# The first steps of a feed-forward stage: bias rows loaded in two parts, the last block's statistics and the next tile's transposes moved earlier

## The reference, cut to what matters

```python
Xd = _quant_dequant_fp8(X)                     # X = layernorm(x), bf16, 2048 x 512
D = Xd @ W0d.T + bias0.astype(jnp.float32)     # 2048 x 1792
D = jax.nn.gelu(D, approximate=False)
Dd = _quant_dequant_fp8(D.astype(bf16))
E = Dd @ W1d.T + bias1.astype(jnp.float32)     # 2048 x 512
x = x + E
```

## Time and profile before

| | us |
|---|---|
| median of 3 runs | 1640.8 (1638.39 to 1643.19) |
| the profiled execution's own time | 1641.23 |
| its span, first to last instruction | 1639.5 |
| PE, DVE, ACT, POOL busy in it | 1485.9, 1267.8, 858.3, 305.9 |

### The profile page before, as it was taken

How to read it: one execution, slowest core, us unless ns; L and a number is a source line. 1 busy time by engine, 2 the same in 40 slices (tenths; PEclk the granted TensorE clock), 3 DMA queues, 4 the chain that set the end, 5 groups by cost and what they waited for, 6 DMA issues and landing times. The chain is left out here.

```text
span 1639.5 us, 29417 instructions
## 1 busy us (share of the span) xinstructions
PE 1485.9 (91%) x11227; PEld 780.1 (48%) x11227; DVE 1267.8 (77%) x2276; ACT 858.3 (52%) x1776; POOL 305.9 (19%) x271
## 2 busy tenths in 40 slices
PE   6999999999999999999999887799999987777695
PEld 4455455455545554555555443344444444443253
DVE  4877876777677677777777786899888886999777
ACT  3554552343424434434334332688888854888552
POOL 0032130011111102010111100011111103789620
PEclk9999999999999999999999998899999999999898
DMA  6287573214231231414132223122232340876402
GB/s 243 83 173 164 128 169 85 78 52 104 58 97 51 64 102 35 130 27 115 51 102 64 52 103 117 24 45 46 45 62 50 59 97 5 154 110 110 76 1 103
DMA packets 317143, 140.73 MB, mean 86 GB/s; under 512 B 265856, under 2 KB 290560, under 8 KB 316800
## 3 DMA queue, kind: packets, MB, share of 16 engines
q1 hardware_dynamic: 273936, 98.14, 28.3%
q10 hardware_dynamic: 43120, 41.42, 8.3%
HBM read 66.13 MB, written 11.53 MB: 47 GB/s over the span
## 5 line engine op out<-in xcount | busy, mean ns | idle before, releaser
L638 PE MATMUL xp<-WO,OT 128*128 128x512 f16 x1536 | 340.4, 382 | 4.1 <-DVE X L925 4.1
L599 PE MATMUL pj<-XT,WQ 128*128 128x512 f16 x1536 | 338.9, 380 | 5.5 <-DVE WQ L284 4.9
L638 PEld LDWEIGHTS xp<-WO,OT 128*128 128x128 f16 x1536 | 148.3, 98 | 187.3 <-issue 16.2
L599 PEld LDWEIGHTS pj<-XT,WQ 128*128 128x128 f16 x1536 | 148.1, 98 | 181.6 <-issue 7.1
L756 ACT ACTIVATE E<-E 128x512 f32<-128x512 f32 x64 | 40.2, 628 | 300.8 <-DVE E L902 300.8
L1163 PE MATMUL db<-W0T,XD 128*128 128x448 f16 x768 | 156.7, 363 | 15.9 <-DVE XD L1361 11.0
L925 DVE SCALAR_TENSOR_TENSOR X<-xp,X 128x512 f32<-128x512 f32 x128 | 88.2, 689 | 91.1 <-PE xp L638 90.1
L1181 PE MATMUL eb<-W1T,DT 128*128 128x512 f16 x672 | 149.2, 382 | 4.2 <-ACT eb L1268 4.2
L573 POOL TENSOR_TENSOR VW<-VW,XB 128x1024 f32<-128x1024 f32 x14 | 33.0, 2356 | 615.0 <-DVE VW L102 615.0
L862 DVE SCALAR_TENSOR_TENSOR QT<-pj,QT 128x512 f16<-128x512 f32 x128 | 87.9, 687 | 70.8 <-ACT QT L726 70.8
L1163 PEld LDWEIGHTS db<-W0T,XD 128*128 128x128 f16 x768 | 75.7, 100 | 94.6 <-DVE XD L1361 12.0
(11 more groups left out here) (239 smaller groups left out, 2465.7 us busy)
## 6 DMA issues: line engine op xcount, KB each, us to landing
W0T<-in_L_xattn_wo ACTq DMA_DIRECT2D x15, 1024.0 KB, 5.5
W0T<-in_L_xattn_wq SPq DMA_DIRECT2D x9, 1024.0 KB, 5.5
W0T<-in_L_xattn_wq ACTq DMA_DIRECT2D x7, 1024.0 KB, 5.6
X<-in_x SPq DMA_DIRECT2D x4, 1024.0 KB, 7.6
out<-X SPq DMA_DIRECT2D x8, 512.0 KB, 3.6
XB<-in_L_ffn_W ACTq DMA_DIRECT2D x28, 128.0 KB, 3.0
w0t<-XB ACTq DMA_DIRECT2D x7, 512.0 KB, 7.4
w1t<-W0T ACTq DMA_DIRECT2D x7, 512.0 KB, 7.9
```

Source lines behind the costliest of these rows:

```text
L599: last = pe.matmul(bank[:, :], w, src[:, b, k, tokens], start=n == 0, stop=n == 3 * KC - 1)
L638: last = pe.matmul(xp[i % 2][:, :], OT[:, a, j, i * P:(i + 1) * P], WO[:, b, j, :], start=n == 0, stop=n == 3 * REP - 1)
```

## The change

1. Each bias is loaded in two transfers: row 0 into partition 0, and the same row into partitions 1 to 127. SP issues the two single rows first (semaphore `row_ld`), then the two others (`b_ld`), then `W1T`. The bias matmuls of tile 0 contract over partition 0 alone and wait for `row_ld`. The first `seed_d` waits for both semaphores.
2. In steps 0 and 1 PE transposes the next tile behind the first quarter of `first_product`, not behind the fourth. ACT's `high_x` and DVE's `low_x` of these steps stand earlier in their streams.
3. The five pieces of block 3 are made in steps -1, 0, 0, 0 and 1. ACT's square root stands in step 0, ahead of the first gelu.
4. In the first attention one semaphore, `sum_step`, takes the place of two.

The core of the diff:

```diff
+                 "exp_done pj_hi e_hi ot_hi max_done sub_done sum_step p_done pj_lo e_lo ot_lo x_acc "
             def sums(cur, jp):
-                at = count(cur, 2, jp + 1)
-                dve.wait_ge(S["exp_done"], at)
-                dve.reduce_sum(ST[:, 1, jp, :], E[:, jp, :, :], AX.X).then_inc(S["sum_done"], 1)
-                dve.wait_ge(S["sum_done"], at)
-                dve.reciprocal(ST[:, 2, jp, :], ST[:, 1, jp, :]).then_inc(S["rcp_done"], 1)
+                dve.wait_ge(S["exp_done"], count(cur, 2, jp + 1))
+                dve.reduce_sum(ST[:, 1, jp, :], E[:, jp, :, :], AX.X).then_inc(S["sum_step"], 1)
+                dve.wait_ge(S["sum_step"], count(cur, 4, 2 * jp + 1))
+                dve.reciprocal(ST[:, 2, jp, :], ST[:, 1, jp, :]).then_inc(S["sum_step"], 1)
...
         @block.sync
-            sp.dma_start(B0[:, :], b0.partition_broadcast(P)).then_inc(S["b_ld"], 16)
-            sp.dma_start(B1[:, :], b1.partition_broadcast(P)).then_inc(S["b_ld"], 16)
+            for row, b in ((B0, b0), (B1, b1)):
+                sp.dma_start(row[0:1, :], b.partition_broadcast(1)).then_inc(S["row_ld"], 16)
+            for rest, b in ((B0, b0), (B1, b1)):
+                sp.dma_start(rest[1:P, :], b.partition_broadcast(P - 1)).then_inc(S["b_ld"], 16)
...
-                        pe.matmul(db[q][:, 0:NQ], ones[:, :], B0[:, q * NQ:(q + 1) * NQ], start=True, stop=False)
+                        pe.matmul(db[q][:, 0:NQ], ones[0:1, :], B0[0:1, q * NQ:(q + 1) * NQ], start=True, stop=False)
...
-                    pe.wait_ge(S["b_ld"], 32)
+                    pe.wait_ge(S["row_ld"], 32)
+
+                soon = fixed(i) in (0, 1)
                 if live(i):
-                    first_product(i, range(4))
+                    first_product(i, range(1) if soon else range(4))
                 if live(nxt):
                     transpose_x(nxt)
+                if soon:
+                    first_product(i, range(1, 4))
...
             def seed_d(i, qs):
                     if fixed(i) == 0 and q == 0:
                         act.wait_ge(S["b_ld"], 32)
+                        act.wait_ge(S["row_ld"], 32)
...
                     x_times_rec(after)
+                if fixed(i) == 0:
+                    stats_x(act, 3)
+                if fixed(i) in (0, 1):
+                    high_x(nxt)
...
-                if live(nxt) and fixed(i) != -1:
+                if live(nxt) and fixed(i) not in (-1, 0, 1):
                     high_x(nxt)
...
-                if fixed(i) == X3_STEPS[1]:
-                    stats_x(act, 3)
...
                     quant_x(after)
+                if fixed(i) == -1:
+                    x_moments(dve, 3)
+                if fixed(i) in (0, 1):
+                    low_x(nxt)
+                if fixed(i) == 0:
+                    x_statistics(dve, 3)
                 if live(hidden):
                     off_grid_d(hidden)
...
+                if fixed(i) == 0:
+                    x_normal(dve, 3)
                 if live(i):
                     amax_d(i, 1)
...
                     scales_d(i)
+                if fixed(i) == 0:
+                    x_amax(dve, 3)
                 if live(hidden):
                     low_d(hidden, 0)
                     low_d(hidden, 1)
-                for n, piece in enumerate(x_pieces):
-                    if fixed(i) == X3_STEPS[n]:
-                        piece(dve, 3)
+                if fixed(i) == 1:
+                    x_scales(dve, 3)
```

More of the change, by code:

```diff
@@ L429, in attention0 @@
         names = ("o_hi o_lo sc_done pj_done pt_done pv_done xp_done "
-                 "exp_done pj_hi e_hi ot_hi max_done sub_done sum_done rcp_done p_done pj_lo e_lo ot_lo x_acc "
+                 "exp_done pj_hi e_hi ot_hi max_done sub_done sum_step p_done pj_lo e_lo ot_lo x_acc "
                  "wb_ld wb2_ld wa_done wstep ww_done wcut wbits wm_done wsum wqs_done wq_done wt_done wt_hi wt_lo w_st "
@@ L905, in sums @@
             def sums(cur, jp):
-                at = count(cur, 2, jp + 1)
-                dve.wait_ge(S["exp_done"], at)
-                dve.reduce_sum(ST[:, 1, jp, :], E[:, jp, :, :], AX.X).then_inc(S["sum_done"], 1)
-                dve.wait_ge(S["sum_done"], at)
-                dve.reciprocal(ST[:, 2, jp, :], ST[:, 1, jp, :]).then_inc(S["rcp_done"], 1)
+                dve.wait_ge(S["exp_done"], count(cur, 2, jp + 1))
+                dve.reduce_sum(ST[:, 1, jp, :], E[:, jp, :, :], AX.X).then_inc(S["sum_step"], 1)
+                dve.wait_ge(S["sum_step"], count(cur, 4, 2 * jp + 1))
+                dve.reciprocal(ST[:, 2, jp, :], ST[:, 1, jp, :]).then_inc(S["sum_step"], 1)
             def normalise(cur, jp):
-                dve.wait_ge(S["rcp_done"], count(cur, 2, jp + 1))
+                dve.wait_ge(S["sum_step"], count(cur, 4, 2 * jp + 2))
                 dve.tensor_tensor(E[:, jp, :, :], E[:, jp, :, :], ST[:, 2, jp, :].unsqueeze(2).to_broadcast([P, BB, SEQ]),
@@ L1055, in _, with ffn0 @@
             last_slot(later(LAST, 2), later(LAST, 3))
-def ffn0(nc, sb, pb, sem, X, ident, ahead_of_ffn0, x_scales, x_buffers, x_sems, w1t_dram, b0, b1,
+def ffn0(nc, sb, pb, sem, X, ident, ahead_of_ffn0, of_x, x_buffers, x_sems, w1t_dram, b0, b1,
          loads1, ln_stats, SH, queries1, kv1, loaded1):
     with ExitStack() as ph:
-        W0T, XB, w0_ld, x_pieces, stats_x = ahead_of_ffn0
-        xs, xr, xstep = x_scales
+        W0T, XB, w0_ld, (x_moments, x_statistics, x_normal, x_amax, x_scales), stats_x = ahead_of_ffn0
+        xs, xr, xstep = of_x
         stats_vector, stats_scalar = ln_stats
@@ L1087, in ffn0 @@
         eb = pb(ph, "eb")
-        names = ("w1_ld b_ld kvw_hi kvw_lo qw_hi "
+        names = ("w1_ld b_ld row_ld kvw_hi kvw_lo qw_hi "
                  "xt_done xt_hi xt_lo d_done ones_done gelu_done d_seeded e_seeded da_done dstep dw_done dcut dbits dm_done dsum "
@@ L1092, in ffn0 @@
         block = ph.enter_context(nc.Block())
-        X3_STEPS = (0, 1, 2, 3, 4)
         LN_STEPS = {TILES: (0, 1), TILES + 1: (2,)}
@@ L1176, in second_product @@
                 else:
-                    pe.matmul(eb[:, :], ones[:, :], B1[:, :], start=True, stop=False)
+                    pe.matmul(eb[:, :], ones[0:1, :], B1[0:1, :], start=True, stop=False)
                 pe.wait_ge(S["dt_done"], count(i, 32, 32))
```

## The result

The changed kernel took 1647.39 us in the median of 10 runs (1644.59 to 1652.38), the kernel before 1641.42 in 10 runs beside it (1638.39 to 1643.9). The ratio is 1.0041, 95% interval 1.0028 to 1.0054: some 6 us slower. Forecast were 1646.3 us and +5.5.

A forecast was written before the change was run, and what follows sets the result against it. It took ACT's chain with DVE, 18.81 us per tile, as setting the pace. T(0) 1041.0 plus 95.25 gave T(5) 1136.3, +5.5 us, so 1646.3 us; likeliest case 1642.5 to 1653, with Rival A 1630.5 to 1652.

The forecast's parts named there:

- T(0): Start of tile 0's scaling (`d_times_rec`) on ACT in feed-forward 0: 1029.43 before, forecast 1041.0.
- T(5): Start of tile 5's scaling on ACT in feed-forward 0: 1130.84 before, forecast 1136.3, +5.5 us.
- pieces: Block 3's moments, statistics, normalising, largest values and scales, moved off the ACT and DVE chain: 6.2 us less from T(0) to T(5).
- transposes: Next tile's transposes within the first products: `low_x` leaves DVE's path, four transposes precede the fourth quarter; -0.2 us on T(0).
- single rows first: PE's first bias matmul needs only row 0 and starts at 1010.4, 2.9 us earlier.
- 127 rows on one engine: First `seed_d` waits for 127 rows on one DMA engine, 83 in 100; T(0) becomes 1041.0, against 1026.3 without waiting.
- The bound: From T(5) on, PE's chain and that of ACT with DVE keep pace, so T(5) moves the stage's end equally.
- L: Landing time of the 127 bias rows: forecast 1036.1, bounds 1033.0 and 1045.3, break-even 1030.6.
- The semaphore of the softmax: First attention's register instructions move from output split to sums in 21 slots: 0, with 1 us either way.
- Rival A: The 127 rows go to all engines, landing near 1014.5: -9.3 us, 1631.5; 17 in 100, together with Rival C.
- Rival B: One engine at the slow rate, packets at 0.184 and 0.083 us: +14.7, 1655.5; surroundings from +10 up, 10 in 100.
- Rival C: Moved pieces delay something: nothing with one engine, up to 2.9 us with all, leaving -6.4; 17 in 100 with Rival A.

The follow-up runs named there:

- e1: The changed kernel with the 127 other rows of each bias in two transfers, of 112 and 15 partitions; 1630.36 us, ratio 0.9932 against before.
- e5: e1 with the five pieces of block 3 back in steps 0 to 4; 1637.01 us, ratio 0.9969 against before.
- e6: e1 with transposes, `high_x` and `low_x` of tiles 1 and 2 where the kernel before has them; 1628.82 us, ratio 0.9921 against before.
- e2: The changed kernel with both biases loaded whole as before, 128 partitions each; transposes and pieces stay moved; 1634.14 us, ratio 0.9949 against before.
- e8: e1 with tile 1's bias put in by PE's matmul instead of four seeds of ACT; 1630.65 us, ratio 0.9927 against before.
- e7: The changed kernel, its 127-row transfers kept, with tile 1's bias put in by PE's matmul instead of ACT's seed; 1631.54 us, ratio 0.9936 against before.
- e3: The kernel before with biases loaded as 1 and 127 rows and the one softmax semaphore; pieces and transposes unmoved; 1655.83 us, ratio 1.0084.

## Why the prediction was right

The mechanism held: the 127 rows went over one engine, the first seed waited for them with all of tile 0 behind it, and the moved pieces shortened T(0) to T(5). The four parts of the change, each from a pair of kernels that differ in it alone, and what the prediction's steps gave them, in us on T(5):

| part | from | measured | forecast |
|---|---|---|---|
| pieces | e1 against e5 | -6.66 | -6.2 |
| transposes | e1 against e6 | +0.39 | -0.2 |
| single rows first | e1 against e2 | -3.11 | -2.9 |
| 127 rows on one engine | changed against e1 | +15.77 | +14.7 |
| sum | | +6.39 | +5.4 |

The change itself moved T(5) by +6.46, so the parts add up; the medians moved by 5.97. The forecast +14.7 is T(0) of 1041.0 less the 1026.3 without the wait; the prediction's +5.5 is the 5.4 here, rounded on the way.

- *The bound.* T(5) and the end do move together: from T(5) to the stage's end it was 224.08 us before and 223.98 after. In e1 to e8 it was 1.4 to 1.8 us less, about what one stretch at a lower clock costs (1.5 us, below).
- *The pieces.* T(0) to T(5) was to be 95.25 and is 94.83. Of the 1.2 us that I left on the chain 0.8 are there. The same holds where no long wait for the rows covers it: T(0) is 18.87 in e1 with the pieces moved and 18.86 in e5 without, and T(0) to T(5) 94.86 against 101.53.
- *The transposes* had the wrong sign, +0.39 for -0.2. In the changed kernel the wait for the rows hides their part of T(0), so the forecast did not depend on it.
- *The wait for 127 rows.* L is 1037.4 on the clock of before, where 1036.1 stood. The large packets were priced right (0.138 us, and 0.136 measured; 17.6 us for the 127 of them, and 17.3). The fixed part was right too: the first small packet starts at 1030.3, 19.3 us after the issue at 1011.02, which leaves 2.0 beside the 17.3, for 2.2 forecast. The undersized term is the 127 small rows, 7.7 us forecast and 9.7 measured, from 1030.3 to L. The DMA packets of four stretches after, 1030.3 to 1031.4, 1034 to 1036, 1038 to 1039 and, for the sum, 1030.3 to 1040 us, show it:

```profile
DMA packets 26, 0.03 MB, mean 24 GB/s; under 512 B 0, under 2 KB 26, under 8 KB 26
...
DMA packets 54, 0.75 MB, mean 373 GB/s; under 512 B 0, under 2 KB 29, under 8 KB 29
...
DMA packets 19, 0.43 MB, mean 434 GB/s; under 512 B 0, under 2 KB 4, under 8 KB 4
...
DMA packets 234, 3.17 MB, mean 327 GB/s; under 512 B 1, under 2 KB 128, under 8 KB 128
```

  The 1 KB packets start at 24 a us, 0.042 us each. At that rate 127 would take 5.4 us, less than my 7.7. Once `W1T` is under way they fall to 4 a us, which adds 4.3. The trace doesn't name the engine of a packet, but `W1T`'s end shows whose it is. From 1042.6 to 1047.9 us only five of its packets of 28 KB are left, one after another at one engine's rate and share:

```profile
DMA packets 5, 0.14 MB, mean 27 GB/s; under 512 B 0, under 2 KB 0, under 8 KB 0
...
q1 hardware_dynamic: 5, 0.14, 6.3%
```

  So the sixteenth of `W1T` that lies on the rows' engine shares it with them and ends last. `W1T` lands at 1045.8 on the clock of before, where the prediction had 1045. But my sum had `W1T` behind the rows, not among them. The price of a small packet was too high and this sharing was left out; the two errors go against each other, and that L came within 1.3 us is luck to that extent. The signs named in the prediction have it too: the small rows landed 28.7 us after their issue, beyond the 20 to 27 given.
- *From the landing to T(0)* 5.06 us, forecast 4.9.
- *The semaphore of the softmax* shows no cost in the loop: PE's score matmuls start 0.77 us later after than before at 38 us and 0.78 later at 912 us. The rest of the 2.60 comes in the last slots; 1.26 of it is one group of matmuls at a lower clock (48 `xp` matmuls in 11.79 against 10.53 us; the granted clock from 935 to 955 us was 0.91 after and 0.99 before). A cost in those last slots isn't excluded by these two executions alone, but e7, with the same semaphore, reached the barrier at 1007.95, and before at 1007.80.
- *Rival A* was wrong for this kernel, and e1 and e7 show what it would have brought: T(5) -9.31 and -9.33, forecast -9.3. That their times, 1630.36 and 1631.54, also lie near its 1631.5 is in part luck, since they are 12.4 and 11.5 below before. *Rival B* would have had 0.184 us for a packet. *Rival C* cost nothing measurable, as the intervals of e1, where DVE has no spare 15 us, show.

e1's median lies 12.4 us below before, and T(5) explains 9.3 of it. All seven kernels timed in turn came out lower against before than T(5) says, by 1.0 us (e3) to 4.5 (e6). Between the two profiled executions it is 11.6 us (1641.23 and 1629.66), and the stage has 11.1 of them (347.12 and 336.01). Of the stage's 11.1, 9.3 are T(5) and another 1.5 us lie in its last product, PE's timeline of before and then of e1:

```profile
1341.97 10.73 PE L1181 MATMUL eb<-W1T,DT 128*128 128x512 f16 x42 [3.00 <-ACT eb L1268]
```

```profile
1334.84 9.24 PE L1182 MATMUL eb<-W1T,DT 128*128 128x512 f16 x42 [2.68 <-ACT eb L1274]
```

The granted clock of the 6 us around its start (the windows' columns as in the earlier trace rows) was 0.72 before and 1.00 in e1, a part at the lower level, 1.2 GHz, against none:

```profile
1341.00:1347.00 6.00, 5.03 (x17) 2.04 (x18) 5.83 (x13) 3.95 (x8) 1.15 (x1) 0.72 0.00 0
```

```profile
1334.00:1340.00 6.00, 5.17 (x24) 2.37 (x25) 5.86 (x13) 3.82 (x8) 1.15 (x1) 1.00 0.00 0
```

The changed kernel has the slow one too (10.75), all the others the fast one, in one execution each. PE had waited 3.00 us before and 2.88 after, and 2.64 to 2.72 in the fast ones but for e3, which had waited 3.05 and kept its clock. So the wait's length alone doesn't decide it. What does is open, and so is the rest of e1's 12.4.

## What to carry to other kernels

Splitting off row 0 made the first user 3 us earlier and left 127 rows, which went over one DMA engine at 26 GB/s and landed 29 us after their issue; split the rest at a multiple of 16 (112 and 15, each about 3 us). A load off the critical path is judged by its own first user: here that was a seed for the *next* tile, 13 us into the stage, and with this one user moved (e7) the slow rows were harmless. Moving the statistics into stretches where DVE had to wait anyway took 6.7 us off the chain. A wait that is not on the chain, as PE's 7.91 us, was worth nothing when it shrank, and moving the transposes to shrink it cost 0.4 us.

## What the runs showed of the hardware

SP itself is held when a transfer on one engine is under way. Its timeline after answers to the earlier trace rows; the second of the two transfers of 127 rows takes 7 us to issue, and `W1T` behind it 12.4, where before each took 0.43:

```profile
1010.35 0.61 SPq L1128 DMA_DIRECT2D SH<-in_L_ffn_bias  x2
1011.02 7.32 SPq L1130 DMA_DIRECT2D SH<-in_L_ffn_bias  x2
1018.38 12.41 SPq L1131 DMA_DIRECT2D W1T<-w1t  x1
```

So SP is busy until 1030.8, 0.5 us after the last large packet has moved, and `W1T` lands 30.0 us after its issue instead of 12.9. It was so in e3 (6.55 for the pair, 12.58) and e7 (7.20, 12.38), and not in e1, where all four issues took 1.68 us. What holds it isn't shown. Here SP had nothing else to do until the first DMA transpose; in a kernel where it had, this would have been a second wait that no engine's row of the kernel before could have shown.
